# Causal masks added to attention scores as two 64x64 products onto 64 rows each, in place of two 64x128 products onto all 128 rows

## The chip, the cores and the metric

One NeuronCore of a Trainium2 chip runs the whole program. The metric is the time of one execution on the device in microseconds (us); the number to compare is the median of several runs. TensorE (PE in the profile, PEld for its weight loads) multiplies, VectorE (DVE) reduces and scans, ScalarE (ACT) does exponentials and copies, GpSimd (POOL) works on data in SBUF, and the sync engine (SP) issues transfers.

## The reference

For x of 4096 rows and 256 channels it computes

```
h   = layernorm(x)
q, k, v = split(h @ Wqkv + b)                     # 16 heads of 16 channels
att = softmax(q k^T / 4 + causal_mask) v          # causal_mask: -10000 above the diagonal
stp = a decaying state (16x16 per head, own rate per cell), updated by v k^T, read by q
y   = alpha * att + (1 - alpha) * stp             # alpha: a small gate network on h
x   = x + y @ out_w + out_b
out = x + fp8_quantised_linear(layernorm(x))
```

The change concerns the causal mask alone. With 4096 rows, the kernel needs it only for blocks of scores that lie on the diagonal.

## The kernel before

The program has three stages. First the projections of all rows are computed and written to memory in the layouts that attention needs. Then the main loop does attention and the recurrence (the state) together. Last come the gate, the output projection and the quantised layer.

**The main loop** runs once for each of four groups of 4 heads. The 4096 queries are cut into 8 chunks of 512 (`CH`); a group goes through the chunks in the order 3, 4, 5, 6, 7, 2, 1, 0 (`ORDER`). A *tile* is one chunk of queries against 128 keys, for the 4 heads of the group: chunk c has 4(c+1) tiles, a group 144, and the loop 576. The last four tiles of each chunk lie on the diagonal: there the causal mask is needed, and of the 512 queries only 512, 384, 256 and 128 are computed. 32 of a group's 144 tiles are such diagonal tiles, 128 in all.

Every tile is made of these steps on PE, in the order that `TILE_ORDER = "SUMMSSMMSV"` writes down:

- **S, a score product** (`scores`, L1160): keys on the 128 output rows, queries on up to 512 columns. Head h sits on partitions 0 to 49 (even h, side 0) or 64 to 113 (odd h, side 1), so that it uses 50 of the upper or lower 64 rows of the array. ACT takes the exponential from PSUM into `probs` (L1279). There are three PSUM banks for S, so the fourth S waits until the exponential of the first is done.
- **M, a product for the maxima** (`max_scores`, L1126): the same scores the other way round, queries on the rows and keys on the columns. Two M stand side by side, one for each side of the array, and DVE reduces both at once into `pmax` (L1329). They work for a chunk that comes later. There are two pairs of banks, so a pair waits for the reduction before the last one.
- **V, the values** (`values`, L1181): for the tile before, four products in float32, each onto 17 rows of its own strip of 32 output rows.

Recurrence steps come in between on some tiles: `burst` (L1211 to L1219), `lag` (L1194), turns (L1246, L1253), and a scan on DVE (L1364). M runs two chunks ahead: the M of the first two chunks of the first group are done before the loop starts, and in the last 36 tiles of the last group no M is left.

**The mask.** Scores are masked by adding a product onto them in PSUM. The mask is a 128x128 matrix in bfloat16, and a head may use only its own 64 rows of the array. So the sum over 128 rows is cut into two products of 64 rows, `half` 0 and 1, that run one after the other onto the same 128 output rows:

```
def add_mask(bank, side, mask):
    rows = slice(side * SIDE, (side + 1) * SIDE)
    for half in range(2):
        mm = pe.matmul(bank, ident_sides[rows, half, :], mask[rows, half, :], ...)
```

`ident_sides[rows, half, :]` is 64 rows of the 128x128 identity, so half 0 adds the mask to output rows 0 to 63 and zeros to the rest, and half 1 the other way round. A diagonal tile has four masked S (`mask_kq_sides`). An M is masked (`mask_qk_sides`) when its key block is the queries' own chunk (`blk == c`); both M of a pair are then masked, and they have 128, 256, 384 or 512 columns. By the code there are 256 such pairs: 16 ahead of the loop, 44 in diagonal tiles and 196 in other tiles.

Of the kernel before, what the change touches and what calls it, by code (L numbers as in the profile page):

```python
# [13 lines left out]
P = 128  # L14
# [18 lines left out]
SIDE = P // SIDES  # L33
# [85 lines left out]
def max_item(s, n):  # L119

    c = ORDER[s]
    side, n = 1 - n % SIDES, n // SIDES
    pair, j, blk = n // (TPC * (c + 1)), n // (c + 1) % TPC, n % (c + 1)
    return pair, side, j, blk, CH if blk < c else (j + 1) * P
# [167 lines left out]
def preln_attention_ffn_kernel(nc, x, wqkv, bqkv, out_w, out_b, w_static, lam, gamma, gate_w1,  # L292
                               gate_b1, gate_w2, gate_b2, ffn_wt, ffn_b, out):
    ctx = ExitStack()
    with ctx:
        def sb(name, shape, dt=F32, where=ctx):
            return where.enter_context(nc.sbuf_tensor(name, shape, dt))
# [4 lines left out]
        PS = ctx.enter_context(nc.psum_tensor("PS", [P, 8, CH], F32))  # L302
# [13 lines left out]
        ident_sides = sb("ident_sides", [P, SIDES, P], BF16)  # L316
        mask_qk_sides = sb("mask_qk_sides", [P, SIDES, P], BF16)
        mask_kq_sides = sb("mask_kq_sides", [P, SIDES, P], BF16)
# [540 lines left out]
        with att:  # L859
# [22 lines left out]
            with nc.Block() as block:  # L882
# [226 lines left out]
                def _(pe):  # L1109
                    def max_scores(g, s, n):  # L1110

                        c = ORDER[s]
                        if n == 0:
                            n_parts = 16 * STACK_LOADS
                            pe.wait_ge(loaded[f"q{c}"], g * n_parts + n_parts)
                            if s in FIRST_USE:

                                pe.wait_ge(loaded["k_" + FIRST_USE[s]], g * n_parts + n_parts)
                        pair, side, j, blk, width = max_item(s, n)
                        rows = slice(side * SIDE, side * SIDE + KS)  # L1120
                        item = MAX_AT[s] + n
                        bank = S_BANKS + item // SIDES * SIDES % M_BANKS + side
                        keys = K_first if s < FIRST_USERS and blk < FIRST else K_st

                        pe.wait_ge(max_done, g * (N_MAX // SIDES) + item // SIDES + 1)
                        mm = pe.matmul(PS[:, bank, 0:width], Q_st[rows, c, pair, j * P:(j + 1) * P],  # L1126
                                       keys[rows, pair, blk * CH:blk * CH + width], start=True, stop=(blk < c))
                        if blk == c:
                            mm = add_mask(PS[:, bank, j * P:(j + 1) * P], side, mask_qk_sides)
                        mm.then_inc(max_ready, 1)  # L1130

                    def add_mask(bank, side, mask):
                        rows = slice(side * SIDE, (side + 1) * SIDE)
                        for half in range(2):
                            mm = pe.matmul(bank, ident_sides[rows, half, :], mask[rows, half, :], start=False, stop=(half == 1))  # L1135
                        return mm

                    def wait_emptied(group, before, turns_before):
# [11 lines left out]
                    def scores(g, s, kt, h, bank):  # L1150

                        c = ORDER[s]
                        pair, side = h // SIDES, h % SIDES
                        rows = slice(side * SIDE, side * SIDE + KR)
                        r = max(kt - TPC * c, 0)
                        if kt == 0 and h == 0:
                            pe.wait_ge(shift_loaded[s % 2], g * (SHIFTED * NCH // 2) + SHIFTED * (s // 2 + 2))
                        keys = K_first if s < FIRST_USERS and kt < FIRST * TPC else K_st

                        mm = pe.matmul(PS[:, bank, 0:CH - r * P], keys[rows, pair, kt * P:(kt + 1) * P],  # L1160
                                       Q_st[rows, c, pair, r * P:CH], start=True, stop=(kt < TPC * c))
                        if kt >= TPC * c:
                            mm = add_mask(PS[:, bank, 0:P], side, mask_kq_sides)
                        mm.then_inc(scores_ready, 1)

                    def values(g, s, kt):
# [57 lines left out]
                    def walk(group, steps, emptied, turns_before):  # L1224
                        for step in steps:
                            kind, g, s = step[0], group + step[1], step[2]
                            if kind == "max":
                                max_scores(g, s, step[3])
                            elif kind == "scores":
                                wait_emptied(group, emptied[step[:5]], turns_before)  # L1230
                                scores(g, s, step[3], step[4], step[5])
                            elif kind == "values":
                                values(g, s, step[3])
                            elif kind == "burst":
                                wait_emptied(group, emptied[step[:3]], turns_before)
                                burst(g, s, step[3])
                            elif kind == "lag":
                                if emptied[step[:4]]:
                                    wait_emptied(group, emptied[step[:4]], turns_before)
                                lag(g, s, step[3], step[4])  # L1240
                            elif kind == "shift_turn":

                                pe.wait_ge(folded, g * NCH + s + 1)
                                if emptied[step[:3]]:
                                    wait_emptied(group, emptied[step[:3]], turns_before)
                                pe.transpose(PS[0:GH * TPC, step[3], 0:P], neg_max[:, s % 2, :], ident[:, :])\  # L1246
                                    .then_inc(shift_turned, 1)
                            elif kind == "out_turn":

                                pe.wait_ge(out_evacuated, g * NCH + s + 2)  # L1250
                                wait_emptied(group, emptied[step[:3]], turns_before)
                                for j in range(TPC):
                                    mm = pe.transpose(PS[:, step[3], j * P:(j + 1) * P], o_t[:, s % 2, j * P:(j + 1) * P],  # L1253
                                                      ident[:, :])
                                mm.then_inc(out_turned, 1)
# [499 lines left out]
```

## Time and profile before

| | |
|---|---|
| median of 3 runs | 2127.93 us (2119.26 to 2133.13) |
| profiled execution | 2120.3 us, of which the span from first to last instruction is 2118.6 us |
| PE, matmul busy | 1800.1 us, 85% of the span |
| DVE busy | 1558.5 us, 74% |
| ACT busy | 1368.7 us, 65% |
| POOL busy | 1153.0 us, 54% |
| main loop | from about 274 to 1942 us |

An engine's busy share is an average over stages. A matmul's end in the records is modelled, and products on different rows or columns of the array overlap in time, so that a high PE share does not say that the array is at its peak. In the timeline the start of a product is what to read: the distance from one start to the next is what a product costs the stream.

### The profile page before, as it was taken

Reading aid. Unit: us, or ns where it says so; the run is one execution under the profiler, and the core shown is the slowest. Engines: PE = TensorE matmul, PEld = TensorE weight load, DVE = VectorE, ACT = ScalarE, POOL = GpSimd, SP = SyncE. Lnnn points to the kernel's source line nnn. Section 1 sums busy time; section 2 is a strip of 40 time slices with the busy share of each in tenths; the row PEclk is TensorE's granted clock in tenths of the full one; section 3 lists DMA queues with packets and bytes.
Section 4 is the critical chain, followed back from the end, with each engine's and each line's share of the span. In section 5 each row is a group of like instructions: output and inputs, shape, how many; then the busy total and the mean of one; then the engine's idle time right before and its main releaser. Section 6 shows DMA issues by size and latency. Waiting matters only on the chain. (4 is left out here: it accounts for less than half of the span.)

```text
span 2118.6 us, 47123 instructions
## 1 busy us (share of the span) xinstructions
PE 1800.1 (85%) x15280; PEld 718.8 (34%) x15280; DVE 1558.5 (74%) x1712; ACT 1368.7 (65%) x2853; POOL 1153.0 (54%) x1130
## 2 busy tenths in 40 slices
PE   5995589999999899999989999999899998986743
PEld 3552133333334333333343323333433233322632
DVE  5334988888788778887878888878888788601767
ACT  2441067777776777777767777777677777875221
POOL 3102246565666566666666666666567757630535
PEclk9996589999999999999999999999999999998865
DMA  4778041232122412321224124112242121102601
GB/s 127 194 192 198 12 89 59 67 78 64 50 67 66 95 57 69 79 66 50 66 63 99 56 65 94 55 47 79 59 107 67 46 75 45 51 8 57 190 0 79
DMA packets 144582, 163.60 MB, mean 77 GB/s; under 512 B 63440, under 2 KB 91088, under 8 KB 144336
## 3 DMA queue, kind: packets, MB, share of 16 engines
q1 hardware_dynamic: 141952, 158.74, 27.9%
q8 instruction: 131, 2.15, 0.4%
q10 hardware_dynamic: 2384, 1.77, 0.3%
q14 instruction: 115, 0.94, 0.2%
HBM read 122.00 MB, written 38.01 MB: 76 GB/s over the span
## 5 line engine op out<-in xcount | busy, mean ns | idle before, releaser
L1329 DVE TENSOR_REDUCE pmax<-PS 128x2 f32<-128x1024 f32 (+3 forms) x1152 | 1252.5, 1131 | 268.1 <-PE PS L1126 218.2
L1279 ACT ACTIVATE probs<-PS 128x512 f32<-128x512 f32 (+3 forms) x2304 | 1149.5, 566 | 441.9 <-PE PS L1160 336.5
L1160 PE MATMUL PS<-Q_st,K_st 50*128 50x512 f16 (+3 forms) x1408 | 419.0, 360 | 65.9 <-ACT stp_sb L1308 24.7
L1126 PE MATMUL PS<-K_st,Q_st 48*128 48x512 f16 (+3 forms) x1408 | 349.2, 360 | 23.4 <-DVE pmax L1329 22.1
L1181 PE MATMUL PS<-probs,V_g 128*17 128x512 f32 (+3 forms) x2816 | 339.2, 554 | 0.0
L1044 POOL TENSOR_TENSOR v_exp<-v_exp,k_rows 128x512 f32<-128x512 f32 x256 | 321.1, 1287 | 16.7 <-DMA v_exp<-qkv_t 13.7
L1160 PE MATMUL PS<-Q_st,K_first 50*128 50x512 f16 (+3 forms) x896 | 281.6, 382 | 38.8 <-ACT stp_sb L1308 15.2
L1126 PE MATMUL PS<-K_first,Q_st 48*128 48x512 f16 (+2 forms) x896 | 240.6, 413 | 54.3 <-DVE pmax L1329 40.8
L1077 POOL TENSOR_TENSOR state<-ends,q_rows 128x516 f32<-128x516 f32 x256 | 276.1, 1111 | 0.0
L1072 POOL COPY carry<-ends 128x4 f32<-128x4 f32 x64 | 12.1, 189 | 457.1 <-DVE ends L1364 457.1
L1160 PEld LDWEIGHTS PS<-Q_st,K_st 50*128 50x128 f16 x1408 | 113.6, 93 | 418.4 <-ACT probs L1279 296.2
L1054 POOL TENSOR_TENSOR pairs<-pairs,v_exp 128x512 f32<-128x512 f32 x128 | 165.7, 1295 | 135.2 <-ACT pairs L1288 135.2
L1181 PE MATMUL PS<-probs,V_first 128*17 128x512 f32 (+3 forms) x1792 | 230.2, 586 | 0.0
L1160 PEld LDWEIGHTS PS<-Q_st,K_first 50*128 50x128 f16 x896 | 73.3, 94 | 289.1 <-ACT probs L1279 203.3
L1219 PE MATMUL PS<-state,sum_e 128*32 128x128 f32 x2048 | 142.9, 408 | 0.0
L1288 ACT ACTIVATE pairs<-v_exp,decay 128x256 f32<-128x256 f32 x256 | 132.5, 519 | 0.3
L1135 PE MATMUL PS<-mask_kq_sides,ident_sides 64*128 64x128 bf16 x1024 | 124.7, 215 | 0.0
L1126 PEld LDWEIGHTS PS<-K_st,Q_st 48*128 48x128 f16 x1408 | 84.4, 93 | 75.4 <-DVE pmax L1329 68.5
L1135 PE MATMUL PS<-mask_qk_sides,ident_sides 64*128 64x128 bf16 x1024 | 104.9, 222 | 0.0
L1219 PEld LDWEIGHTS PS<-state,sum_e 128*32 128x32 f32 x2048 | 90.7, 123 | 20.0
L1364 DVE TENSOR_TENSOR_SCAN ends<-decay_x,sums 128x516 f32<-128x516 f32 x64 | 79.3, 1240 | 22.4 <-POOL sums L1065 22.4
L621 PE MATMUL PS<-xn_t,wqkv_sb 128*128 128x512 f32 x192 | 94.2, 652 | 1.8 <-ACT xn_t L678 1.8
(163 smaller groups left out, 1569.8 us busy)
## 6 DMA issues: line engine op xcount, KB each, us to landing
v_exp<-qkv_t SPq DMA_DIRECT2D x256, 256.0 KB
qkv_t<-proj SPq DMA_DIRECT2D x24, 512.0 KB, 3.7
qk_parts<-parts SPq DMA_DIRECT2D x16, 512.0 KB, 5.3
Q_st<-qk_parts SPq DMA_DIRECT2D x192, 32.0 KB, 3.4
v_rows<-vaug SPq DMA_DIRECT2D x32, 136.0 KB, 6.1
xin<-x SPq DMA_DIRECT2D x8, 512.0 KB, 6.0
k_rows<-qkv_t SPq DMA_DIRECT2D x16, 256.0 KB, 4.7
q_rows<-qkv_t SPq DMA_DIRECT2D x16, 256.0 KB, 6.8
```

The source lines that it names most:

```text
L621: mm = pe.matmul(PS[:, 2 + u % 4, :], w, xn_t[:, par, c, :], start=(c == 0), stop=(c == HALF - 1))
L1044: pool.tensor_tensor(v_exp[:, n % RING], v_exp[:, n % RING], k_rows[:, b % 2], ALU.mult)\
L1054: pool.tensor_tensor(pairs[:, B % 2, k:k + 2], pairs[:, B % 2, k:k + 2], v_exp[:, slot:slot + 2, 1:CH:2], ALU.add).then_inc(pair_made, 1)
L1077: pool.tensor_tensor(state[:, B % 2, k].rearrange("p (c e) -> p c e", e=STEP4), ends[:, B % 2, k].unsqueeze(2).broadcast_to([P, BLOCKS + 1 ...
L1126: mm = pe.matmul(PS[:, bank, 0:width], Q_st[rows, c, pair, j * P:(j + 1) * P], keys[rows, pair, blk * CH:blk * CH + width], start=True, st ...
L1135: mm = pe.matmul(bank, ident_sides[rows, half, :], mask[rows, half, :], start=False, stop=(half == 1))
L1160: mm = pe.matmul(PS[:, bank, 0:CH - r * P], keys[rows, pair, kt * P:(kt + 1) * P], Q_st[rows, c, pair, r * P:CH], start=True, stop=(kt < T ...
L1181: mm = pe.matmul(PS[h * VW:h * VW + VN, O_BANK, r * P:CH], v[:, kt, h * VN:(h + 1) * VN], probs[:, tile % P_SLOTS, h, 0:CH - r * P], start ...
L1219: mm = pe.matmul(rows(e), sum_e[:, half, q * BATCH + k, e, :], own[:, 1 + e:1 + e + STEP4 * (BLOCKS - 1) + 1:STEP4], start=False, stop=(k ...
L1279: act.activation(probs[:, tile % P_SLOTS, h, 0:CH - r * P], PS[:, step[5], 0:CH - r * P], ACT.Exp, scale=SCORE_SCALE).then_inc(exp_done, 1)
L1288: act.activation(pairs[:, B % 2, s % BATCH, :], v_exp[:, s % RING, 0:CH:2], ACT.Identity, scale=decay[:, 0, col:col + 1]).then_inc(u_scale ...
L1329: dve.tensor_reduce(pmax[:, s % 2, pair * TPC + j:GH * TPC:PAIRS * TPC, blk], PS[:, bank:bank + SIDES, 0:width], AX.X, ALU.max).then_inc(m ...
```

## The change

Each half of the mask is added to the 64 output rows that it reaches, by a product of 64 rows by 64 columns of the array. Both halves use the same 64x64 identity block. The number of products and the columns that each streams (128) stay as they were; the second half no longer comes onto the same output rows as the first.

```
-def add_mask(bank, side, mask):
+def add_mask(bank, cols, side, mask):
     rows = slice(side * SIDE, (side + 1) * SIDE)
     for half in range(2):
-        mm = pe.matmul(bank, ident_sides[rows, half, :], mask[rows, half, :], start=False, stop=(half == 1))
+        mm = pe.matmul(PS[half * SIDE:(half + 1) * SIDE, bank, cols], ident_sides[rows, 0, 0:SIDE],
+                       mask[rows, half, :], start=False, stop=True)
     return mm
```

The two callers pass the bank's number and the columns: `slice(j * P, (j + 1) * P)` in `max_scores`, `slice(0, P)` in `scores`. Nothing moves on any engine: the order of all instructions is the same, and only the output rows of the mask products differ. This is PE's order within a diagonal tile of 256 columns, from its second pair of M, here a masked one of 128 columns, to the values. Before:

```order
L1125 REGISTER_ALU
L1126 MATMUL PS<-K_st,Q_st 128x128
L1135 MATMUL PS<-mask_qk_sides,ident_sides 128x128 x2
L1126 MATMUL PS<-K_st,Q_st 128x128
L1135 MATMUL PS<-mask_qk_sides,ident_sides 128x128 x2
L1142 REGISTER_ALU
L1160 MATMUL PS<-Q_st,K_first 128x256
L1135 MATMUL PS<-mask_kq_sides,ident_sides 128x128 x2
L1181 MATMUL PS<-probs,V_first 17x384 x4
```

The same place now (the lines behind `add_mask` have moved down by one):

```order
L1125 REGISTER_ALU
L1126 MATMUL PS<-K_st,Q_st 128x128
L1135 MATMUL PS<-mask_qk_sides,ident_sides 64x128 x2
L1126 MATMUL PS<-K_st,Q_st 128x128
L1135 MATMUL PS<-mask_qk_sides,ident_sides 64x128 x2
L1143 REGISTER_ALU
L1161 MATMUL PS<-Q_st,K_first 128x256
L1135 MATMUL PS<-mask_kq_sides,ident_sides 64x128 x2
L1182 MATMUL PS<-probs,V_first 17x384 x4
```

The masks (L1135) stand between the two M of a pair and between S and the values as they did; their outputs have 64 rows (the first number) where they had 128.

## Rows read from the trace of the kernel before

**Rows 1.** The page: PE's busy time, and its granted clock in 40 slices

```profile
PE 1800.1 (85%) x15280; PEld 718.8 (34%) x15280; DVE 1558.5 (74%) x1712; ACT 1368.7 (65%) x2853; POOL 1153.0 (54%) x1130
...
PEclk9996589999999999999999999999999999998865
```

**Rows 2.** Stretches before and in the loop: length, busy PE, PEld, DVE, ACT, POOL, clock

```profile
192.00:274.00 82.00, 46.18 (x209) 11.90 (x205) 74.78 (x76) 3.91 (x7) 25.10 (x22) 0.50 0.23 57
274.00:1942.00 1668.00, 1528.45 (x14236) 564.06 (x14235) 1286.52 (x1296) 1257.42 (x2683) 1015.79 (x1003) 0.99 0.24 65
```

**Rows 3.** Timeline of PE over one plain tile: start, length, operation, count

```profile
900.76 0.39 PE L1160 MATMUL PS<-Q_st,K_st 50*128 50x512 f16 x1
...
900.99 0.59 PE L1160 MATMUL PS<-Q_st,K_st 50*128 50x512 f16 x2
...
901.83 0.39 PE L1160 MATMUL PS<-Q_st,K_st 50*128 50x512 f16 x1
902.15 1.05 PE L1181 MATMUL PS<-probs,V_g 128*17 128x512 f32 x8
903.13 0.39 PE L1160 MATMUL PS<-Q_st,K_st 50*128 50x512 f16 x1
```

**Rows 4.** Timeline of ACT over the same tile, with its idle time before

```profile
901.18 2.06 ACT L1279 ACTIVATE probs<-PS 128x512 f32<-128x512 f32 x4 [0.31 <-PE PS L1160]
```

**Rows 5.** Timeline of DVE over the same tile

```profile
901.40 2.36 DVE L1329 TENSOR_REDUCE pmax<-PS 128x2 f32<-128x1024 f32 x2 [0.82 <-PE PS L1126]
```

**Rows 6.** Groups of instructions of PE: the mask products

```profile
L1135 PE MATMUL PS<-mask_kq_sides,ident_sides 64*128 64x128 bf16 x1024 | 124.7, 215 | 0.0
L1135 PE MATMUL PS<-mask_qk_sides,ident_sides 64*128 64x128 bf16 x1024 | 104.9, 222 | 0.0
```

**Rows 7.** Timeline of PE where values come before the turn of the outputs

```profile
1080.61 1.05 PE L1181 MATMUL PS<-probs,V_g 128*17 128x512 f32 x8
1081.59 0.66 PE L1253 MATMUL PS<-ident,o_t 128*128 128x128 f32 x4
1082.18 0.39 PE L1160 MATMUL PS<-Q_st,K_st 50*128 50x512 f16 x1
```

**Rows 8.** Timeline of PE over a diagonal tile of 128 columns

```profile
1090.93 0.84 PE L1181 MATMUL PS<-probs,V_g 128*17 128x384 f32 x8
1091.70 0.23 PE L1160 MATMUL PS<-Q_st,K_st 50*128 50x128 f16 x1
...
1091.77 0.27 PE L1135 MATMUL PS<-mask_kq_sides,ident_sides 64*128 64x128 bf16 x2
...
1092.68 0.63 PE L1181 MATMUL PS<-probs,V_g 128*17 128x256 f32 x8
```

**Rows 9.** Timeline of PE over a diagonal tile of 384 columns

```profile
1087.27 0.33 PE L1160 MATMUL PS<-Q_st,K_st 50*128 50x384 f16 x1
...
1087.44 0.27 PE L1135 MATMUL PS<-mask_kq_sides,ident_sides 64*128 64x128 bf16 x2
...
1088.29 0.33 PE L1160 MATMUL PS<-Q_st,K_st 50*128 50x384 f16 x1
1088.47 0.27 PE L1135 MATMUL PS<-mask_kq_sides,ident_sides 64*128 64x128 bf16 x2
1088.67 1.05 PE L1181 MATMUL PS<-probs,V_g 128*17 128x512 f32 x8
```

**Rows 10.** Timeline of PE over a tile with a masked pair of M

```profile
908.72 0.39 PE L1160 MATMUL PS<-Q_st,K_st 50*128 50x512 f16 x1
...
909.46 0.29 PE L1126 MATMUL PS<-K_st,Q_st 48*128 48x256 f16 x2
909.58 0.28 PE L1135 MATMUL PS<-mask_qk_sides,ident_sides 64*128 64x128 bf16 x4
909.79 0.39 PE L1160 MATMUL PS<-Q_st,K_st 50*128 50x512 f16 x1
910.11 1.05 PE L1181 MATMUL PS<-probs,V_g 128*17 128x512 f32 x8
```

**Rows 11.** Waits in the loop: total us, times, longest

```profile
DVE pmax L1329 <- PE PS L1126: 215.7, 243, 4.0
```

More of the change, by code:

```diff
@@ L1128, in max_scores @@
                         if blk == c:
-                            mm = add_mask(PS[:, bank, j * P:(j + 1) * P], side, mask_qk_sides)
+                            mm = add_mask(bank, slice(j * P, (j + 1) * P), side, mask_qk_sides)
                         mm.then_inc(max_ready, 1)
-                    def add_mask(bank, side, mask):
+                    def add_mask(bank, cols, side, mask):
                         rows = slice(side * SIDE, (side + 1) * SIDE)
                         for half in range(2):
-                            mm = pe.matmul(bank, ident_sides[rows, half, :], mask[rows, half, :], start=False, stop=(half == 1))
+                            mm = pe.matmul(PS[half * SIDE:(half + 1) * SIDE, bank, cols], ident_sides[rows, 0, 0:SIDE],
+                                           mask[rows, half, :], start=False, stop=True)
                         return mm
@@ L1162, in scores @@
                         if kt >= TPC * c:
-                            mm = add_mask(PS[:, bank, 0:P], side, mask_kq_sides)
+                            mm = add_mask(bank, slice(0, P), side, mask_kq_sides)
                         mm.then_inc(scores_ready, 1)
```

## The prediction, made before the changed kernel had run

> **What bounds the kernel now.** I read the page first: PE has matmuls in flight for 85% of the span, DVE and ACT are well below, and PE's clock is at its full level except at the two ends [rows 1]. The stretches then say where the time is: the loop takes 1668.0 of the span's 2118.6 us, with PE covered for 1528.45 of them, DVE 1286.52 and ACT 1257.42, at a granted clock of 0.99 (the full level, 2.4 GHz) [rows 2]. The loop is where all masks but 16 pairs stand. So the question is what sets a tile's length.
>
> The timeline of a plain tile shows it. S starts at 900.76 and the next two S at 900.99 and behind it, 0.22 us apart, which is what 512 columns cost the stream. The fourth S comes only at 901.83, because it needs the bank of the first, whose exponential starts at 901.18, and ACT is then at work for 2.06 us on four of them. The values follow at 902.15 and the next tile's S at 903.13: a period of 2.38 us, a loop S, exponential, S, values, S with PE on it all the way [rows 3, 4]. DVE's two reductions take 2.36 us of the same period [rows 5], so it has next to nothing in reserve in plain tiles, and yet it waits 215.7 us for M over the loop [rows 11], because bursts and turns stretch other tiles. The reader is to see that PE's order is one chain: what is put between S and the values lengthens the tile, unless PE would have waited there.
>
> **What the change removes.** The mask products are 2048 instructions [rows 6], and all stay. Each streams its 128 columns as before; only half of the array's columns are used. If the two halves, on different columns of the array, start together, as the four products of the values on four strips do (eight of them in 1.05 us [rows 3]), one of two masks disappears from the chain: 0.06 us for each of 1024 masked products. That is taken from widths: S to its mask costs 0.17 for 384 columns [rows 9] and 0.07 for 128 [rows 8], so about 0.12 for 256 and 0.22 for 512; a mask, also 128 columns, costs 0.06. The weight load of a mask lies under the products before it now and costs nothing.
>
> **What the change adds.** Before, S, M and masks all use the array as 64 rows by 128 columns, and only the values leave that form. What leaving it costs is in the trace. The fourth S goes to the values in 0.32 us where S to S takes 0.22: 0.10 on top [rows 3]. From values to S: 512 columns take 0.98 [rows 3], 384 take 0.77 [rows 8]; 128 columns are 0.21, so 0.98 - 4 x 0.21 = 0.14 does not belong to the columns. Nor do the rows of the array have to change for it: values (128 rows, strips of 32 columns) to a turn of outputs (128 rows, 128 columns) takes the same 0.98, and the turn to S, where only the rows change, again more than four products of 128 columns ask for (0.59) [rows 7]. A mask before the values shows it too: its first product is at 1088.47, the values at 1088.67, 0.20 for two masks of 0.06 [rows 9]. So every change of form seen here costs 0.08 to 0.14 us, in either direction, whatever the width; I take 0.10. No row shows 64x128 to 64x64 itself. Its price lies between nothing (if a part of the columns counts as the same form) and 0.14; I take 0.10, because the nearest row, values to turn, changes columns alone and pays it.
>
> The Trainium skill has a rule for the step that no row shows: its page "TensorEngine Tiling (Array Packing)", section Key Properties, says that changing the tiling mode, not merely the tile, drains the engine, and by its list of modes 64x64 is not the mode of 64x128. It gives no figure. By that rule with the rows' 0.10 the sum is the one below. The same section says that different tiles run in parallel; with that alone and no drain the sum would be the gain of the first rival.
>
> A change of form has a second price. Today the sides of the array overlap: in a pair both M start at 909.46 and all four masks at 909.58, together [rows 10]. In PE's order the masks of the first M stand ahead of the second M. If the masks are of another form, the second M must wait for them and for two changes.
>
> **The sum, in tiles.** With w for the columns' 0.07, 0.12, 0.17, 0.22 (mean 0.145) and 0.06 for the two halves together:
>
> - A masked S costs w + 0.10 + 0.06 + 0.10, and nothing runs beside it. A diagonal tile is four of them and two plain pairs of M at 0.22. For 384 columns: 4 x 0.43 + 0.44 = 2.16 from S to the values, where it is 1088.67 - 1087.27 = 1.40 [rows 9]. For 128 columns: 4 x 0.33 + 0.44 = 1.76, where it is 1092.68 - 1091.70 = 0.98 [rows 8]. So about +0.75. By the code 68 diagonal tiles have plain M: 51 us.
> - A masked pair of M costs 2w + 0.52 = 0.81 where a plain one costs 0.22; less the little that its masks cost now, +0.5. 44 diagonal tiles have one: 44 x 1.25 = 55 us.
> - 16 diagonal tiles at the end have no M; ACT paces them and the four masked S fit nearly: 16 x 0.2 = 3 us.
> - 196 masked pairs stand in other tiles, where PE waits for ACT before the fourth S. There the mask is free today: S to values is 1.39 with one [rows 10] and 902.15 - 900.76 = 1.39 without [rows 3]. Changed, a pair that may start 0.45 behind the first S waits for its neighbour's end at 0.67, then 0.10 + 0.06 + 0.10 to the second M, w + 0.26 to the fourth S: 1.34 for the mean width against 1.07, +0.27. Where the pair starts late because it had to wait for DVE, as at 909.46, it is 909.46 + 2 x 0.12 + 0.52 = 910.22 against 909.79, +0.43. I take 0.3: 59 us.
> - 16 pairs ahead of the loop: DVE is busy for 74.78 of 82.00 us there and PE at half clock [rows 2], so most is covered: 6 us.
>
> Together 174 us. Against it stand waits that are there anyway and take part of it up: PE is without a product for 1668.0 - 1528.45 = 140 us of the loop, 0.24 a tile, and 308 tiles (128 diagonal, some 180 others) get longer, so 74 us at the very most. As many of these waits are in bursts and turns at other places, I count 45. What DVE's waits (215.7 us) show is that it catches up easily. 174 - 45 = 129, and the profiled execution of 2120.3 becomes 2249; the median of the runs shown lies 7.6 us above the profiled one, so about **2255 us**. What comes next as the bound is PE's own chain, more than before.
>
> **The rivals.** (1) *The 64x64 form costs no change, and the halves run together.* For: the rows stay 64, and the values show that strips of columns run beside each other. Against: every row on a change of columns. Then two or three of the four masks in a diagonal tile are on the chain at 0.06, 112 x 0.16 = 18 us less at most, nothing in the other tiles, where PE waits; about 2113. If DVE, near its limit, takes that back, 2125. It decides if the change of form costs under 0.01 us. Chance 12%: two parts in three of it within 1%, one beyond.
> (2) *The halves don't run together though the form changes.* Then each masked product is 0.06 longer than summed, 1024 x 0.06 = 61 us, of which some 50 show: 2305. For: nothing in the trace shows two strips of 64. Against: the values on four strips. Chance 12%.
> (3) *The changes are paid and the waits hide nearly all.* It would need the diagonal tiles to be set by ACT or DVE; the 0.98 us of the 128-column tile [rows 8] against DVE's 2.36 a tile speaks for some of that, since DVE falls behind there and the next tile waits for it. Fully hidden it gives 2135; chance 3%.
> The forecast's own case has 73%. Its bounds: 2128 + 174 - 74, less again if a change costs 0.08 and the pairs come on time, is about 2180. With nothing hidden and all of PE's work in the chain (240 pairs x 0.54, 128 diagonal tiles x 0.99, from the same prices against overlapped sides) it is 257 us: 2385, which the rows 9 tile contradicts (0.76 of 0.99), so 2350.
>
> **Numbers.** 2255 us. The range is 2165 to 2350: it leaves out rival 1, rival 3 and the tails of the main case, some 2 in 10. About 1% (21 us) is what a measurement of this kernel can tell from no change. Faster by over 1%: 0.04 (a third of rival 1). Within: 0.11 (the rest of it and rival 3). Slower: 0.85.
>
> **What the changed profile would show.** If I am right: two M of a masked pair no longer start together but some 0.4 to 0.5 us apart; S to mask of 384 columns goes from 0.17 to about 0.27; the two halves of a mask start within 0.01; the diagonal tile of 384 columns takes about 2.1 us from S to values, plain tiles keep 2.38; the loop grows from 1668 to about 1795, and the stages outside stay. PE's busy time may grow little or fall, as changes of form are gaps. If the gap at the mask is absent, rival 1 holds. I am also wrong if PE, with more gaps, is granted its lower clock (1.2 GHz, 0.50 in the rows) for long in the loop; today that happens hardly at all there (0.99). Then it is worse than summed. If the gaps are there and the loop grows by less than 60 us, the waits hid more than I count.

## The result, and the profile after

The changed kernel takes 2384.69 us (median of 4 runs, 2382.29 to 2385.85) against 2125.11 us (4 runs, 2119.26 to 2133.13): ratio 1.1217, 95% interval 1.1177 to 1.1258. It is slower, as forecast, by 260 us where 127 had been forecast, and it lies above the range's end of 2350.

The page, for [rows 1]:

```profile
PE 2112.6 (89%) x15280; PEld 755.4 (32%) x15280; DVE 1571.4 (66%) x1712; ACT 1400.7 (59%) x2853; POOL 1151.5 (48%) x1130
...
PEclk9995679997997999979968999999899999986675
```

The numbers of instructions are the same. PE's busy time is up by 312 us, where the prediction had said that it may grow little or fall. The second line is the one to look at: before, the clock stands at 9 in every slice that lies wholly in the loop [rows 1]; now 7s, 8s and 6s are strewn along it. The stretch ahead of the loop and the loop itself, with the columns of [rows 2]:

```profile
192.00:278.90 86.90, 55.35 (x209) 14.62 (x209) 75.09 (x76) 3.94 (x8) 24.54 (x22) 0.50 0.22 53
...
278.90:2208.70 1929.80, 1833.36 (x14231) 600.07 (x14231) 1298.59 (x1296) 1289.39 (x2683) 1013.96 (x1003) 0.92 0.21 56
```

The loop has grown by 262 us, what is ahead of it by 5. DVE, ACT and POOL run the same instructions as before; in the loop DVE is busy for 12 us more and ACT for 32. The granted clock of the loop is 0.92, where it was 0.99 [rows 2].

The diagonal tile of 384 columns, the very tile of [rows 9], at full clock:

```profile
1224.60 0.33 PE L1161 MATMUL PS<-Q_st,K_st 50*128 50x384 f16 x1
1224.87 0.24 PE L1135 MATMUL PS<-mask_kq_sides,ident_sides 64*64 64x128 bf16 x2
1225.04 0.39 PE L1126 MATMUL PS<-K_first,Q_st 48*128 48x512 f16 x2
1225.27 0.32 PE L1161 MATMUL PS<-Q_st,K_st 50*128 50x384 f16 x1
1225.52 0.24 PE L1135 MATMUL PS<-mask_kq_sides,ident_sides 64*64 64x128 bf16 x2
1225.70 0.33 PE L1161 MATMUL PS<-Q_st,K_st 50*128 50x384 f16 x1
...
1226.62 0.24 PE L1135 MATMUL PS<-mask_kq_sides,ident_sides 64*64 64x128 bf16 x2
1226.79 1.05 PE L1182 MATMUL PS<-probs,V_g 128*17 128x512 f32 x8
```

S to its mask is 0.27 us (it was 0.17), mask to the next product 0.17, of which 0.06 is the mask: the way in costs 0.10 and the way back 0.11 to 0.12. This holds all over the trace: at full clock, the medians from S to its mask are 0.16, 0.21, 0.26 and 0.32 us for 128, 256, 384 and 512 columns, 0.10 above what the columns cost, and from a mask to the next S or M 0.17 whatever its width. The two halves are one group of 0.24 us, the length of one, so they do run together. From the first S to the values it is 2.19 us, where it was 1.40.

The tile of [rows 10], with a masked pair of M:

```profile
1003.70 0.39 PE L1161 MATMUL PS<-Q_st,K_st 50*128 50x512 f16 x1
...
1004.44 0.28 PE L1126 MATMUL PS<-K_st,Q_st 48*128 48x256 f16 x1
1004.65 0.24 PE L1135 MATMUL PS<-mask_qk_sides,ident_sides 64*64 64x128 bf16 x2
1004.83 0.28 PE L1126 MATMUL PS<-K_st,Q_st 48*128 48x256 f16 x1
1005.04 0.24 PE L1135 MATMUL PS<-mask_qk_sides,ident_sides 64*64 64x128 bf16 x2
1005.21 0.39 PE L1161 MATMUL PS<-Q_st,K_st 50*128 50x512 f16 x1
1005.53 1.05 PE L1182 MATMUL PS<-probs,V_g 128*17 128x512 f32 x8
```

The second M starts 0.39 us behind the first (0.4 to 0.5 had been forecast), where both started together, and the fourth S comes 0.77 us behind the first M, where it was 0.33. The tile is 0.44 us longer.

DVE now waits for M as follows, for [rows 11]:

```profile
DVE pmax L1330 <- PE PS L1126: 371.5, 311, 4.7
```

These spacings and waits are as forecast. What was not is the clock. Chunk 6 has 28 tiles, the same in each group, with the same instructions. These are their stretches in the first three groups, after the change:

```profile
474.89:570.60 95.71, 91.85 (x703) 28.95 (x699) 67.81 (x64) 62.51 (x129) 52.81 (x52) 0.86 0.29 66
959.72:1055.56 95.84, 91.94 (x703) 28.91 (x699) 67.80 (x64) 62.51 (x129) 52.71 (x51) 0.87 0.27 65
1455.63:1542.06 86.43, 82.51 (x703) 27.48 (x699) 67.69 (x64) 62.17 (x128) 51.89 (x52) 1.00 0.31 73
```

and before:

```profile
446.16:526.18 80.02, 75.49 (x706) 27.07 (x703) 67.05 (x64) 61.16 (x128) 50.17 (x51) 1.00 0.33 78
866.01:946.02 80.01, 75.47 (x706) 27.08 (x703) 67.05 (x64) 61.16 (x129) 50.22 (x51) 1.00 0.34 78
```

At full clock the change costs these 28 tiles 6.4 us (PE's busy time grows by 7.0, so the gaps of the changes are recorded as work); where the clock is granted at 0.86, another 9.3. As the clock has two levels, 1.00 and 0.50, a granted 0.86 means that 2 x 0.14 x 95.7 = 27 us passed at the lower one (1.2 GHz), so a microsecond there costs 9.3 / 27 = 0.35 us. What it does to single products shows in another tile of the same trace, where the clock stood at 0.50:

```profile
1035.24 0.32 PE L1135 MATMUL PS<-mask_kq_sides,ident_sides 64*64 64x128 bf16 x2
1035.49 1.91 PE L1182 MATMUL PS<-probs,V_g 128*17 128x512 f32 x8
```

The eight products of the values take 1.91 us, where they take 1.05 at full clock. If PE's products were the whole chain, a microsecond at the lower level would cost 0.5 us; part of the tile is waits for ACT and DVE, whose instructions take as long as before (an exponential 564 ns on the mean, where it was 566; a reduction 1131 in both).

### The profile page after: what moved, and what is told of

It is laid out like the page before. It is cut to its first block and busy times, and to the rows that moved or that the text cites. A ratio compares the mean times of both kernels' runs of the same rounds, so it can differ in the third digit from the quotient of the medians.

```text
span 2384.1 us, 47123 instructions
## 1 busy us (share of the span) xinstructions
PE 2112.6 (89%) x15280; PEld 755.4 (32%) x15280; DVE 1571.4 (66%) x1712; ACT 1400.7 (59%) x2853; POOL 1151.5 (48%) x1130
## 5 line engine op out<-in xcount | busy, mean ns | idle before, releaser
L1330 DVE TENSOR_REDUCE pmax<-PS 128x2 f32<-128x1024 f32 (+3 forms) x1152 | 1263.8, 1131 | 486.2 <-PE PS L1126 373.7
L1280 ACT ACTIVATE probs<-PS 128x512 f32<-128x512 f32 (+3 forms) x2304 | 1177.7, 564 | 674.8 <-PE PS L1161 427.0
L1161 PE MATMUL PS<-Q_st,K_st 50*128 50x512 f16 (+3 forms) x1408 | 462.8, 383 | 41.7 <-ACT stp_sb L1309 18.9
L1126 PE MATMUL PS<-K_st,Q_st 48*128 48x512 f16 (+3 forms) x1408 | 379.0, 371 | 15.5 <-DVE pmax L1330 14.7
L1182 PE MATMUL PS<-probs,V_g 128*17 128x512 f32 (+3 forms) x2816 | 373.1, 606 | 0.0
L1161 PE MATMUL PS<-Q_st,K_first 50*128 50x512 f16 (+3 forms) x896 | 292.1, 392 | 36.5 <-ACT stp_sb L1309 13.5
L1126 PE MATMUL PS<-K_first,Q_st 48*128 48x512 f16 (+2 forms) x896 | 253.5, 436 | 44.3 <-DVE pmax L1330 29.1
L1135 PE MATMUL PS<-mask_kq_sides,ident_sides 64*64 64x128 bf16 x1024 | 134.4, 259 | 0.0
L1135 PE MATMUL PS<-mask_qk_sides,ident_sides 64*64 64x128 bf16 x1024 | 129.2, 249 | 0.0
L1135 PEld LDWEIGHTS PS<-mask_kq_sides,ident_sides 64*64 64x64 bf16 x1024 | 57.4, 108 | 136.6 <-issue 122.2
```

The source lines that it names most:

```text
L1135: mm = pe.matmul(PS[half * SIDE:(half + 1) * SIDE, bank, cols], ident_sides[rows, 0, 0:SIDE], mask[rows, half, :], start=False, stop=True)
L1182: mm = pe.matmul(PS[h * VW:h * VW + VN, O_BANK, r * P:CH], v[:, kt, h * VN:(h + 1) * VN], probs[:, tile % P_SLOTS, h, 0:CH - r * P], start ...
L1280: act.activation(probs[:, tile % P_SLOTS, h, 0:CH - r * P], PS[:, step[5], 0:CH - r * P], ACT.Exp, scale=SCORE_SCALE).then_inc(exp_done, 1)
L1330: dve.tensor_reduce(pmax[:, s % 2, pair * TPC + j:GH * TPC:PAIRS * TPC, blk], PS[:, bank:bank + SIDES, 0:width], AX.X, ALU.max).then_inc(m ...
```

## The experiments

**One half of the change at a time.** In the first run only the callers' masks of S are narrow:

```
-            mm = add_mask(bank, slice(j * P, (j + 1) * P), side, mask_qk_sides)
+            mm = add_mask_full(bank, slice(j * P, (j + 1) * P), side, mask_qk_sides)
```

with `add_mask_full` as `add_mask` was. In the second it is the other caller, so that only the masks of M are narrow.

> Only the masks of S (512 score products in the 128 diagonal tiles) are added in the 64x64 form; the masks of M keep the 64x128 form. Theory A (each masked product pays two changes of form and loses its overlap with the other side, and on top PE is granted its lower clock for part of the loop, which costs about 0.37 us for each us at that level): the changes give 128 tiles x 0.75 = 96 us, and as the lower clock follows the diagonal tiles most of its 100 us comes along, so about 2290 us, with a clearly lower clock than 0.936. Rival B (no waits hide anything and the clock costs nothing): 128 x 0.99 = 127 us, 2252 us.

Measured: 2215.66 us, ratio 1.0390 (1.0335 to 1.0444) against a kernel before of 2130.86 us, granted clock 0.921.

> Only the masks of M (256 pairs) are added in the 64x64 form; the masks of S keep the 64x128 form. Theory A: 196 x 0.3 + 44 x 0.5 + 6 = 87 us, less some 20 that waits take, and hardly any lower clock, since in three of four such tiles PE streams as much as before: about 2195 us with a clock near 0.93. Rival B: 240 x 0.54 = 130 us, 2255 us. If the two parts of the change don't influence each other, the excesses of this run and of the one with S alone add up to 259 us.

Measured: 2240.73 us, ratio 1.0495 (1.0438 to 1.0552), clock 0.914. The loops of the two, in this order:

```profile
277.50:2040.40 1762.90, 1649.90 (x14231) 565.24 (x14232) 1291.47 (x1296) 1274.23 (x2682) 1015.28 (x1003) 0.97 0.23 61
```

```profile
281.10:2068.90 1787.80, 1674.03 (x14235) 585.65 (x14232) 1290.78 (x1296) 1268.18 (x2682) 1014.14 (x1003) 0.96 0.23 61
```

Neither number was met. The expectation gave the S part nearly all of the lower clock and the M part none; in fact both parts lower it a little (loop 0.97 and 0.96), and only together do they take it to 0.92. The parts, +85 and +110, add up to 195 us and not 260; the sum over the runs, below, puts most of that down to the clock. Rival B, without a price for the clock, expected 2252 and 2255: it is wrong in the first, and in the second it came nearer (by 14 us) than Theory A (2195, by 46).

**The form without the narrow masks.** The masks are full again, and one product of one column with weights of zero stands ahead of them:

```
+    pe.matmul(PS[0:SIDE, bank, cols.start:cols.start + 1], ident_sides[rows, 0, SIDE:P],
+              mask[rows, 0, 0:1], start=False, stop=False)
     for half in range(2):
-        mm = pe.matmul(PS[half * SIDE:(half + 1) * SIDE, bank, cols], ident_sides[rows, 0, 0:SIDE], ...)
+        mm = pe.matmul(PS[:, bank, cols], ident_sides[rows, half, :], mask[rows, half, :], ...)
```

> The kernel before, with its masks in full 64x128 form, and one more product of 64 rows, 64 output rows and 1 column with weights of zero ahead of each masked product's two masks. It adds nothing to the scores; it only makes PE leave the 64x128 form and come back, as often as in the changed kernel. Theory A: the changes of form are the price, not the narrow masks, so it costs what the change costs and, as the two halves of a mask run one after the other again, up to 0.06 us x 1024 more: 2390 to 2440 us. Rival C (the 64x64 masks are slow themselves, for instance by weight loads that no longer lie under other work): 1024 x 0.03 us more than before at most, 2125 to 2160 us.

Measured: 2334.06 us, ratio 1.0953 (1.0888 to 1.1019), clock 0.908. Rival C is gone: 1024 products of a single column, with zeros for weights, cost 203 us when they are of the other form. That is 56 us below the least that Theory A gave, and the timeline shows one reason. The tile of [rows 10]:

```profile
982.74 0.28 PE L1126 MATMUL PS<-K_st,Q_st 48*128 48x256 f16 x1
982.95 0.19 PE L1134 MATMUL PS<-mask_qk_sides,ident_sides 64*64 64x1 bf16 x1
983.07 0.23 PE L1137 MATMUL PS<-mask_qk_sides,ident_sides 64*128 64x128 bf16 x1
983.07 0.28 PE L1126 MATMUL PS<-K_st,Q_st 48*128 48x256 f16 x1
```

From the first M (256 columns, 0.11) to the one column it is 0.21, from there to the mask 0.12. The mask of one side and the M of the other now start together, as they share a form again; in the changed kernel this M had to wait for the mask too. A product of one column in the 64x128 form was not run, so what the added product costs by itself is not known; in the changed kernel, where none is added, the way in and the way back are 0.10 and 0.11 to 0.12 all the same.

**Fewer trips.** In masked pairs of M, both M are issued first and then the masks of both:

```
-    if blk == c:
-        mm = add_mask(bank, slice(j * P, (j + 1) * P), side, mask_qk_sides)
-    mm.then_inc(max_ready, 1)
+    if blk < c:
+        mm.then_inc(max_ready, 1)
+    elif n % SIDES == 1:
+        for b, s_ in ((bank - side + 1 - side, 1 - side), (bank, side)):
+            add_mask(b, slice(j * P, (j + 1) * P), s_, mask_qk_sides).then_inc(max_ready, 1)
```

> The changed kernel with PE's order altered in masked pairs of M: both M first, then the masks of both, so that a pair has two changes of form where it had four and both M run side by side again. Theory A: each of 240 pairs saves its second w (0.145) and two changes (0.22), 88 us, of which waits give back some 20, and a little of the clock returns: about 2310 us. Rival C (narrow masks are slow themselves): no difference, 2385 us.

Measured: 2244.94 us, ratio 1.0521 (1.0467 to 1.0576), clock 0.918. That is 140 us less than the changed kernel, with the same products. The same tile again:

```profile
952.76 0.28 PE L1126 MATMUL PS<-K_st,Q_st 48*128 48x256 f16 x2
952.97 0.25 PE L1137 MATMUL PS<-mask_qk_sides,ident_sides 64*64 64x128 bf16 x4
953.15 0.39 PE L1163 MATMUL PS<-Q_st,K_st 50*128 50x512 f16 x1
```

All four masks are one group, and the S comes 0.39 us behind the M instead of 0.77. The expectation (2310) missed by 65 us. It had the chain right (88 us of stream less 20 for waits; the sum below gives 70) and undervalued what comes back with the clock, which makes the other half.

**Useless work.** In diagonal tiles of 384 columns and fewer, the changed kernel computes each unmasked M twice:

```
+    if again and blk < c:
+        pe.matmul(PS[:, bank, 0:width], Q_st[rows, c, pair, j * P:(j + 1) * P],
+                  keys[rows, pair, blk * CH:blk * CH + width], start=True, stop=True)
```

> The changed kernel with useless work for PE: in diagonal tiles of 384 columns and fewer, each unmasked M is computed twice, into the same bank, the second time over the first. That is 84 tiles with up to two pairs of 0.22 us, some 30 us more for PE's chain. Theory A (about 105 of the change's 259 us come from the lower clock, 322 us of the loop against 37 before, at 0.37 us each): denser columns behind the changes of form give part of the clock back, so the time rises by less than 30 us or falls, to between 2330 and 2395, and the lower clock has clearly less than 322 us of the loop. Rival B (the clock costs nothing): 2415 us.

Measured: 2387.27 us (2367.65 to 2402.58), ratio 1.1205 (1.1120 to 1.1289), clock 0.895. Some 30 us of work were added and the time did not change clear of its spread (2384.69); by the clock's records of the profiled run the lower level took 256 us of the loop, where it was 322. In the tiles that ran at full clock (counted as in the sum below) the chain grew by 24 us, and 66 us less at the lower level, at 0.35 each, give back 23. That is Theory A, though only a part of the clock came back. Rival B's 2415 lies above all four runs. These four say more, since they are the same program with different clocks. Here they are with the fastest and slowest of the 23 runs of the kernel before that were timed beside them:

```
kernel                us        granted clock of the run
useless work          2402.58   0.890
useless work          2393.32   0.895
useless work          2381.22   0.899
useless work          2367.65   0.908
before, slowest       2143.05   0.918
before, fastest       2115.16   0.938
```

The time at the lower level is 2 x (1 - clock) x time. From the last to the first run of the useless work it is 529 against 436 us, for 35 us of time: 0.38 us each. For the kernel before, 351 against 262 us, for 28 us: 0.31 each. A line through all 23 runs gives 0.32. With the 0.35 of the 28 tiles these make 0.31 to 0.38; 0.36 is used below.

**What could have been gained.** The kernel before with half 0 alone, so that the mask of output rows 64 to 127 is left out:

```
-    for half in range(2):
-        mm = pe.matmul(bank, ident_sides[rows, half, :], mask[rows, half, :], start=False, stop=(half == 1))
+    mm = pe.matmul(bank, ident_sides[rows, 0, :], mask[rows, 0, :], start=False, stop=True)
```

> The kernel before with half 0 of each mask alone; the mask of output rows 64 to 127 is left out. 1024 of 2048 mask products are gone. It shows what the change could have gained at most by running the halves side by side at no price (rival 1 of the prediction said 18 us at most). If a mask product is on the chain in two or three of four masked S: 2107 to 2115 us; if waits cover it: within 5 us of before.

Measured: 2128.84 us (12 runs) against 2126.77 (23 runs), ratio 1.0001 (0.9967 to 1.0035). Half of all mask products are gone, and nothing is gained, where 2107 to 2115 had been expected if masks are on the chain. The clocks: 0.915 to 0.920 in eleven of twelve runs, where the kernel before mostly has 0.920 to 0.938. At equal clock it is faster: its 2130.22 at 0.917 stand against the 2143.05 at 0.918 of before, 13 us; the twelve runs lie 15 us below the line through the 23. So the products were worth that much in the chain, and leaving them out lost it again through the clock.

**A version in the old form.** A mask is zero in half of one of its halves. That half streams 64 columns only:

```
 for half in range(2):
+    if mask is mask_qk_sides:
+        cols = slice(0, P) if half == 0 else slice(SIDE, P)
+    else:
+        cols = slice(0, SIDE) if half == 0 else slice(0, P)
-    mm = pe.matmul(bank, ident_sides[rows, half, :], mask[rows, half, :], ...)
+    mm = pe.matmul(bank[:, cols], ident_sides[rows, half, :], mask[rows, half, cols], ...)
```

> The kernel before, form 64x128 throughout, but the half of a mask that is not zero in 64 of its 128 columns only streams these 64: half 1 of a mask of M from column 64 on, half 0 of a mask of S up to column 63. Output as before. Each masked product saves up to 0.03 us of stream: half of what leaving a product out saves, so 5 to 10 us if masks are on the chain, nothing if not.

Measured: 2119.38 us, ratio 0.9965 (0.9935 to 0.9994): 7 us less than before, as expected, though the interval ends just below 1, and the only kernel here below it.

**Order and form apart.** The fewest trips that the order allows, and the same order in full form as its control. To the run with paired M it adds, in diagonal tiles (the places that call `flush` are left out here):

```
+    held = []
+    def flush():
+        for b, s_ in held:
+            add_mask(b, slice(0, P), s_, mask_kq_sides).then_inc(scores_ready, 1)
+        held.clear()
```

The masks of the first S are held until the pair of M behind it is issued, those of the second until the third S is.

> Narrow masks as in the changed kernel, masked pairs of M with both M first, and in diagonal tiles the masks of S moved too: those of the first S behind the next pair of M, those of the second S behind the third S. A diagonal tile then has three trips into the 64x64 form where it had four, and the products of both sides run side by side again. Theory A: for 384 columns S to the values is 0.22 + 0.22 + 0.28, 0.17 + 0.28, 0.22, 0.17 + 0.28 = 1.84 us against 2.19 measured; 112 x 0.35 = 39 us off the 2245 of the run with paired M, and some clock back: about 2195 us. Rival: ACT, which now gets the first S later, takes it back: 2245 us.

Measured: 2208.77 us, ratio 1.0405 (1.0336 to 1.0474), clock 0.922; 2195 had been expected, 2245 by the rival. The tile of [rows 9]:

```profile
1121.67 0.33 PE L1174 MATMUL PS<-Q_st,K_st 50*128 50x384 f16 x1
1121.67 0.55 PE L1126 MATMUL PS<-K_first,Q_st 48*128 48x512 f16 x2
1122.15 0.24 PE L1146 MATMUL PS<-mask_kq_sides,ident_sides 64*64 64x128 bf16 x2
...
1123.43 1.05 PE L1198 MATMUL PS<-probs,V_g 128*17 128x512 f32 x8
```

S to the values takes 1.76 us, 0.43 less than in the changed kernel (0.35 expected).

> The control of the run before: the same order of products and masks, but all masks in full 64x128 form. Theory A: the order alone costs little, since without changes of form the sides overlap in either order: 2120 to 2140 us. If the order itself is worth something, the run before is read against this one.

Measured: 2144.81 us, ratio 1.0103 (1.0040 to 1.0166), 5 us above what was expected. In the trace the growth is in the diagonal tiles; in the other tiles with masked pairs the order alone costs nothing (0.00 us each). That S and its exponential come later in diagonal tiles fits, but was not shown by itself. Between this run and the one before it only the form differs, and it costs 64 us even with the fewest trips.

**The sum over the runs.** Each profiled execution, its excess over the 2118.6 us and clock 0.936 of before, the part that the clock makes (0.36 times the additional time at the lower level), and the rest. The last column gets at the rest without that price. A tile is taken from its first S to the next tile's; only tiles that ran at full clock both in this trace and before are used (485 of 576 in the changed kernel, 500 and more in the others). Their mean growth is taken by kind of tile and multiplied by the tiles of each kind.

```
kernel            span     clock   excess   lower level   of it clock   rest   full-clock tiles
before            2118.6   0.936      -     271               -           -       -
S masks narrow    2214.1   0.921     96     350              28          67      70
M masks narrow    2242.0   0.914    123     386              41          82      86
form only         2327.2   0.908    209     428              57         152     156
M paired          2245.8   0.918    127     368              35          92      99
changed kernel    2384.1   0.883    266     558             103         162     163
grouped           2205.8   0.922     87     344              26          61      65
grouped, full     2143.8   0.931     25     296               9          16      17
```

The rests nearly add up: 67 + 82 = 149 for the parts against 162 for both. The clock's parts don't: 28 + 41 against 103. No run held the clock still and changed nothing else, but the last column does not use the slope and agrees within 7 us. Some 99 us of the changed kernel's growth are left for the clock by it. The order alone makes 16 of the 61 in the grouped run.

By kind of tile, in the changed kernel (each, and all of a kind, in us):

```
kind of tile                        number   forecast each / all   at full clock each / all
diagonal, plain M                       68      0.75 / 51              0.68 / 46
diagonal, one masked pair of M          44      1.25 / 55              1.00 / 44
diagonal, no M                          16      0.2  /  3              0.31 /  5
other, with masked pairs               180      0.33 / 59              0.42 / 75
plain                                  268      0    /  0             -0.03 / -7
ahead of the loop                        -         -    6                 -    5
```

The forecast column sums to 174, the other to 168. Of the time that the loop spent at the lower level, 195 us fall into the 128 diagonal tiles.

## Why the prediction was wrong, by its own steps

**What bounds the kernel** was right: PE's chain from S to the values set the tile, and most of what was put in it came out at the end.

**The price of a change of form** was right: 0.10 was taken, and it is 0.10 in and 0.11 to 0.12 out. The nearest row, where only the columns change, was the right one to take. By the same token rival 1, no price, is out. What it could have gained, 18 us, is at most 13 to 15 in the chain, by the run with half 0 alone, and nothing in that run's time. The rule of the Trainium skill ("TensorEngine Tiling (Array Packing)", section Key Properties, a changed mode drains the engine) agrees with this trace for 64x128 against 64x64, the step that no row had shown: 0.10 in and 0.11 to 0.12 back, in the run with a single column as well.

**The terms of the sum** were right for the single tiles: 2.16 us for the 384-column tile, measured 2.19; 0.76 from the first masked M to the fourth S (0.81 by the mean width), measured 0.77. Added up by halves they gave 87 us for S and 87 for M; the rests are 67 and 82. One was too small: a masked pair outside the diagonal was put at 0.3 us, a choice between 0.27 for a pair that comes on time and 0.43 for one that comes late. It measured 0.42 a tile, 0.38 a pair, 16 us more in all.

**What the waits hide** was too much. 45 us of 174 were taken off; by the tiles at full clock, and with the terms as summed, it is 16 us in the diagonal tiles with M and 7 in the plain ones, about half of it. Together with the masked pairs the tiles made 168 us and not 129, some 40 us of the miss. Why the waits took less was only argued: most may be for the exponential or the reduction of a product of the same chain, which come later by the same amount. PE's time without a product did shrink, from 140 to 96 us of the loop, and that looks like the 45; but in the 28 tiles at full clock the recorded work grew by as much as the tiles did (7.0 against 6.4 us), so this figure does not tell what was hidden.

**The clock** is the step that failed, some 100 us of the miss. The prediction named it last, as something that would make it wrong, with "today that happens hardly at all there (0.99)" as the reason to leave it out of both the sum and the range. But the trace of before had the case in it: the stretch ahead of the loop, where PE worked 46.18 of 82.00 us, ran at 0.50 [rows 2]. The change puts gaps of 0.1 us into PE's stream, four to twelve to a masked tile. The loop's clock fell with them to 0.92, and came back to 0.97 with fewer of them (paired M, the same products) and to 0.93 with work added; what exactly in the stream decides it stays open, and PE's busy share does not tell, as it rose from 92% to 95% of the loop. It was a rival with a price to be had: if the loop's clock fell to 0.9, 2 x 0.1 x 1900 = 380 us at the lower level. At 0.31 to 0.38 us each that is 118 to 144 us. The price can be read from runs of the kernel before alone, whose times vary with their clocks; at the time of the prediction three of its runs had been timed and one clock was known. With 168 us for the tiles and 99 for the clock, the profiled 2118.6 becomes 2386, where 2384.1 was measured.

**Rival 2**, the halves one after the other, is refuted by the groups of two in 0.24 us. **The range's upper end** rested on a bound (257 us of PE's work all exposed) that happens to be as large as the result. It was not that, and its nearness is luck: the tile terms came to 162 to 168, and the clock made up the rest.

## What to carry to other kernels

A product that leaves the array's current form costs its neighbours about 0.1 us on the way in and as much on the way out, whatever it does itself, and it ends the overlap of products on different sides; group products by form, or keep small ones in the form of the large ones even where half of their outputs are zeros. If a change thins PE's stream, price the clock beside the chain: compare runs of the same kernel by granted clock, which gives the cost of a microsecond at the lower level before anything is changed. Do not count idle time of the engine whose chain bounds the kernel as a reserve in full: here about half of what had been counted was there. To tell the chain from the clock in one pair of traces, compare only the tiles that ran at full clock in both.

## What the runs showed of the hardware that had not been expected

The loss of clock does not add up over the parts of a change: S alone 0.920 to 0.923, M alone 0.914 to 0.919, both 0.883 to 0.889, from 0.918 to 0.938 before. It also came with less work: leaving out 1024 mask products of 0.06 us lowered the clock from about 0.93 to 0.917 and ate the 13 us that it saved. And it varies from run to run at the same order of instructions: the kernel before was granted 0.918 to 0.938, and its times go with it, 2143 to 2115 us.
